# Moving the V projection of the next pair of heads into units 1 to 3 of a causal attention

## What is computed

```python
x = x + L0_attn_a(layernorm(x))      # "first attention" in this text
...                                  # ffn, delta rule, ffn, grouped attention, ffn
x = x + L1_attn_b(layernorm(x))      # "second attention"
x = x + L1_ffn(layernorm(x))

# L0_attn_a: q, k, v = h @ w + b ; logits = q k^T / sqrt(128), key > query masked out
#            out = softmax(logits) v @ w_o + b_o
# L1_attn_b: scores = clip(q k^T / sqrt(128), -1024, 1024) + slope[head] * key index, masked
#            out = softmax(scores) v @ w_o
```

## Time and profile before

| | |
|---|---|
| median of 3 runs | 4153.95 us (4151.42 to 4154.89) |
| the profiled execution's own time | 4152.63 us |
| its span | 4150.8 us |
| TensorE busy | 3628.7 us (87%) |
| VectorE busy | 2641.4 us (64%) |
| ScalarE busy | 2304.3 us (56%) |
| GpSimd busy | 871.9 us (21%) |
| mean granted TensorE clock | 0.951 of full speed |
| first attention | about 30 to 955 us of the span |
| second attention | about 3000 to 3975 us of the span |

### The profile page before, as it was taken

One profiled execution on the slowest core, in us unless ns is written; L12 is line 12 of the kernel. 1 busy time (PEld: TensorE's weight loads), 2 busy tenths in 40 slices (PEclk: granted clock), 3 DMA queues, 4 the chain that ended last, 5 costly groups with the idle time before them and its releaser, 6 DMA issues. The chain is left out here.

```text
span 4150.8 us, 64279 instructions
## 1 busy us (share of the span) xinstructions
PE 3628.7 (87%) x22356; PEld 2718.0 (65%) x22356; DVE 2641.4 (64%) x5003; ACT 2304.3 (56%) x4900; POOL 871.9 (21%) x968
## 2 busy tenths in 40 slices
PE   7999999993969977578888888868799999999979
PEld 6999999992848966212222222226788888888968
DVE  5666666666636656376667666614488788887853
ACT  5777677774513324136666666642266676676632
POOL 2232333320414423100000000012122322323210
PEclk9999999996989989789999999999899999999989
DMA  1000000000000000100000000011101101101010
GB/s 59 22 11 21 22 21 22 11 11 31 1 19 1 0 3 17 53 6 14 16 15 8 15 15 11 12 48 61 36 27 36 42 26 36 42 26 42 26 61 21
DMA packets 24601, 100.53 MB, mean 24 GB/s; under 512 B 5316, under 2 KB 6084, under 8 KB 18036
## 3 DMA queue, kind: packets, MB, share of 16 engines
q1 hardware_dynamic: 24356, 97.25, 7.1%
HBM read 84.52 MB, written 12.32 MB: 23 GB/s over the span
## 5 line engine op out<-in xcount | busy, mean ns | idle before, releaser
L1525 ACT ACTIVATE ga5m_pr<-ga5m_E 128x512 f32<-128x512 f32 x1024 | 582.1, 596 | 313.0 <-PE ga5m_E L1447 304.4
L1540 DVE TENSOR_REDUCE ga5m_nm<-ga5m_M 128x1 f32<-128x1024 f32 x512 | 597.6, 1219 | 182.6 <-PE ga5m_M L1433 182.0
L352 POOL TENSOR_TENSOR all_X<-all_X,at_part 128x512 f32<-128x512 f32 x256 | 335.0, 1309 | 994.6 <-ACT at_part L532 994.6
L1447 PE MATMUL ga5m_E<-ga5m_Q,ga5m_K 128*128 128x512 bf16 x1024 | 391.4, 394 | 65.4 <-ACT ga5m_pr L1525 51.7
L1433 PE MATMUL ga5m_M<-ga5m_K,ga5m_Q 128*128 128x512 bf16 x1024 | 318.6, 394 | 132.3 <-DMA ga5m_Q<-in_zrows 68.9
L417 PE MATMUL at_A<-all_ident,at_prob 128*128 128x128 f32 x2304 | 340.6, 275 | 31.5 <-ACT at_prob L540 22.3
L1447 PEld LDWEIGHTS ga5m_E<-ga5m_Q,ga5m_K 128*128 128x128 bf16 x1024 | 97.7, 98 | 409.0 <-ACT ga5m_pr L1525 345.5
L417 PEld LDWEIGHTS at_A<-all_ident,at_prob 128*128 128x128 f32 x2304 | 265.2, 140 | 60.2 <-DVE at_q1l L600 26.8
L616 DVE TENSOR_TENSOR at_pT1l<-at_A,at_pT1h 128x512 fp32r<-128x512 f32 (+1 forms) x384 | 235.7, 642 | 64.5 <-ACT at_pT1h L521 58.0
L1460 PE MATMUL ga5m_O<-ga5m_pr,ga5m_Vu 128*32 128x512 f32 x2048 | 274.5, 614 | 0.0
L1433 PEld LDWEIGHTS ga5m_M<-ga5m_K,ga5m_Q 128*128 128x128 bf16 x1024 | 88.6, 99 | 271.5 <-DVE ga5m_nm L1540 133.1
(11 more groups left out here) (382 smaller groups left out, 10604.4 us busy)
## 6 DMA issues: line engine op xcount, KB each, us to landing
at_raw<-in_pack SPq DMA_DIRECT2D x32, 1027.0 KB, 6.1
at_slope<-in_slopes SPq DMA_DIRECT2D x32, 512.0 KB, 4.1
ga5m_Q<-ga_qs SPq DMA_DIRECT2D x48, 192.0 KB
ga_qs<-ga5s_part SPq DMA_DIRECT2D x6, 512.0 KB
ga5m_K<-ga_ks SPq DMA_DIRECT2D x48, 48.0 KB
all_X<-in_x SPq DMA_DIRECT2D x1, 2048.0 KB, 7.3
tq_raw<-in_gu SPq DMA_DIRECT2D x1, 2048.0 KB, 8.0
hw_wug<-in_ug SPq DMA_DIRECT2D x1, 2048.0 KB, 9.2
```

The source lines that it names most:

```text
L352: nc.gpsimd.tensor_tensor(X[:, t:t + 2, :], X[:, t:t + 2, :], part[(i - 1) % 2][:, :, :], ALU.add).then_inc(added, 1)
L1447: nc.tensor.matmul(Eb[e % 2][:, :], K[slot][:, kt * P:(kt + 1) * P], Q[slot][:, j * SEQ + qh * 512:j * SEQ + qh * 512 + 512], start=True, ...
L1525: nc.scalar.activation(pr[e % NR][:, :], Eb[e % 2][:, :], ACT.Exp, scale=scale).then_inc(e_done, 1)
L1540: nc.vector.tensor_reduce(nm[slot][:, k:k + 1], Mb[k % 2][:, :], AX.X, ALU.max, negate=True).then_inc(nm_done, 1)
```

## The change

The two V groups that a head of the first seven pairs of a sequence (heads 0 to 13 of its 16) carries for the next pair stood in units 3 and 7. In an even head they now stand in units 2 and 3, as the last item of the unit (`late`, behind "pv" or "o"). In an odd head they stand in units 1 and 3, behind "q" or "k" and ahead of "o". The later heads of a sequence are not touched.

```diff
-            out = []
+            out, late = [], []
...
                 if m + 1 < NPAIR and n % PER_B < PER_B - 2:
-                    out += {3: [("v", m + 1, 2 * (n % 2))], 7: [("v", m + 1, 2 * (n % 2) + 1)]}.get(u, [])
+                    if n % 2:
+                        out += {1: [("v", m + 1, 2)], 3: [("v", m + 1, 3)]}.get(u, [])
+                    else:
+                        late = {2: [("v", m + 1, 0)], 3: [("v", m + 1, 1)]}.get(u, [])
...
-            return out
+            return out + late
```

## The result

The changed kernel takes 4220.5 us (median of 4 runs, 4219.65 to 4224.71), the kernel before 4154.42 us in its runs beside it (4 runs, 4151.42 to 4162.53). The ratio is 1.0158, with a 95% interval of 1.014 to 1.0176. The profiled execution took 4221.28 us with a span of 4219.5. The forecast was 4222, with a range of 4192 to 4245.

What follows compares the result with a forecast made beforehand. TensorE was full in the first attention; a chain from A to unit 3's transposes plus TensorE's work paced second-attention pairs. 46.4 + 8.4 + 1 + 12 = 67.8 us on 4153.95 gave 4222, range 4192 to 4245.

Steps and rivals of the forecast that it cites:

- The pair, 3.29 us: Second attention: each of 13 pairs of heads gets 2.30 + 0.99 = 3.29 us longer, 42.8 us in all.
- from A to A: A is when VectorE ends an odd head's unit 7 minimum; only then are slope and next raw weights fetched.
- the transposes 2.30 us later: Second attention, even heads: V waits for late weights ahead of unit 3's scores, so unit 3's transposes start 2.30 us later.
- 0.99: Second attention, unit 3's transposes to the next A: one boundary loses 0.39 us, unit 1 gains 1.38, so +0.99 a pair.
- The boundary is VectorE's chain: Unit 7 to next unit 0, second attention: VectorE's work holds the transposes, so removing 1.38 us of V saves only 0.39.
- Head 0 of the second attention, 4.0: Start of the second attention: transposes 3.0 us later through late weights, plus 0.99, so 4.0 us.
- The clock, 12 us: Second attention: three in four of 14 waits end at half clock, 7.5 dips more at 1.6 us, +12 us.
- The first attention, 8.4 and 1: First attention: +0.30 us at each of 28 boundaries, 8.4 us, and 1 us for possibly late weights in head 0.
- V did not fill the pause: Rival, second attention: moved V runs while TensorE waits anyway, saving 8 us, to 4146; chance 0.07.
- the boundaries are not the whole: Rival: weights come in time and only the boundaries cost, 21 us, to 4175; chance 0.06.
- the clock did not go further: Rival, second attention: boundary pauses also bring half clock, two dips per pair, 40 us in place of 12, 4250; chance 0.10.

Runs made afterwards that it cites:

- early raw weights: Raw weights fetched ahead of a pair's second slope in the second attention: changed kernel so edited 4160.4 us, kernel before so edited 4123.96 us.
- V early in unit 2 alone: Against the kernel before, only an even head's first V group moves, from unit 3 to the end of unit 2: 4181.74 us.
- unit 7 empty: Changed kernel, but even heads have their V groups in units 3 and 4, so unit 7 has none: 4187.67 us.
- spare work: Changed kernel with early raw weights plus an unused VectorE instruction in unit 7: 4264.86 us; with GpSimd's add cut to 8 columns, 4222.07 us.

## Why the prediction was right

**The pair, 3.29 us.** Right. In the 13 pairs of the term the distance from A to A grew by 56.5 us in all; 10 dips more (12 instead of 2) take 16 of it at 1.6 each, and the chain from A to the weights was 0.21 us shorter on average (12.93 in place of 13.14, nearly all of it the transfer), which gives back 2.8. That leaves 43.3, or 3.33 a pair (forecast 42.8). The two parts were seen apart: the transposes 2.30 us later, and 0.93 for 0.99 in the rest.

**The boundary is VectorE's chain.** Right, and shown from three sides: an empty unit 7 alone brings the stall, a spare instruction lengthens it by nearly its own length, and with a second V group it is gone. The prediction's split hid how large the boundary is: its 0.99 holds one boundary of a pair. Of the other, the 1.38 of V stand inside the 2.30, and the 0.39 only made the wait for the weights longer. Where nothing waits for weights, the two come to about 1.9 us a pair, as the kernels with early raw weights show.

**Head 0 of the second attention, 4.0.** Right: from its first scores to the A behind head 1 it took 55.27 in place of 51.24 us.

**The clock, 12 us.** Right by the count within two: 12 of 14 waits ended in a dip, 9 more than before (7.5 forecast). Four pauses of which three had a dip were a thin basis, and part of the hit is luck: with 14 waits of 2.5 us in place of 2.7 the kernel with V early in unit 2 alone had dips at 6. In the kernel that the Trainium skill describes (page "TensorE: Matmul & The Clock Gate", section "HAM oscillation — how this bites in real kernels") every wait for the next tile's data, drawn there as longer than most of these, ended in a dip. The traces here agree for 12 of 14 waits, but not where 6 of 14 did. What decides between a dip and none at the same length of pause stays open here.

**The first attention, 8.4 and 1.** 8.6 in place of 9.4, but not by the forecast's terms. In the first sequence a pair grew by 0.29, in the second by 0.55: one of the two boundaries there cost nothing. That is the one before unit 0 of an even head, which has one more item in the first sequence (the "c" of the listing, 0.76 us); that this item fills the place of the V is likely, and no run tests it. So it is 21 × 0.28 = 5.9, not 28 × 0.30. Head 0, which waited 1.95 us for the weights, cost 1.1 (23.58 in place of 22.51 from its first scores to those of head 1), as forecast. Some 1.4 of the 8.6 lie ahead of the first scores (18.3 in place of 16.9), where the change moves nothing and where the ten kernels here lie between 16.9 and 19.8.

**The sum.** 67.8 forecast, 66.1 by the medians and 68.7 by the two spans. It is closer than its terms, and that is luck: the clock took some 2 us more than forecast, the shorter chains gave back nearly 3, and the first attention's boundaries took 2.5 less. The rivals are decided by the same rows: V did not fill the pause (a wait of 2.57 us ahead of it), the boundaries are not the whole (about half of the 66), and the clock did not go further, as the stalls of 1.08 us at the boundaries left it alone: with early raw weights those stalls and one wait in head 0 are what is left of the added waiting, and there is no dip.

## What to carry to other kernels

Before work is taken out of the longest step of an engine, see what stands behind it on the other engines: here 1.38 us of matmuls in unit 7 ran in the shadow of VectorE's chain, and taking them out shortened the boundary by 0.4 us only. Before work is moved to an earlier place, compare the moment at which its inputs are ready with the moment at which the engine now gets there: in an ordered list everything behind the work waits with it. And where a wait ends with a transfer, look in the list of the engine that issues it for what stands ahead: exchanging two transfers was worth 28 us, and with both V groups in the longest unit 44.

## What the hardware showed

Two things had not been expected. An instruction of VectorE that reads two tiles in SBUF (slope and minimum of 1024 columns) took 2.22 us when GpSimd's add of 1.26 us had begun 0.13 ahead of it, and 1.23 otherwise: it waited for nearly the whole add (0.96 on average over 32). The Trainium skill, page "SBUF — State Buffer", section "SBUF: two separate sides", says that of such an instruction and one of GpSimd that reads SBUF, the one that starts first shuts the other out for its whole length. The trace agrees, with 2.18 for 1.23 on average and 1.23 again once the add was cut.

And dips of the clock do not go by the length of the pauses alone: 3 of 15 at 1.5 us on average (before), 2 of 15 at 1.55 (unit 7 empty), 6 of 14 at 2.5 (V early in unit 2), 12 of 14 at 2.7 (after), 12 of 32 at 2.2 and 27 of 32 at 3.2 (spare work, with the short and the whole add), and none at the stalls of 1.08 us. With V early in unit 2 alone, one wait of 1.83 us had a dip behind it, and one of 3.45 had none.
